# First mixture of experts: gate and up as three fp32r products, with the weights split on the fly

## The reference, cut to what matters

```python
x = x + tanh(g_xattn[0]) * xattn0(layernorm(x), ctx, ...)
# first mixture, per token: e = argmax(sigmoid(h @ router_w))
#   y = score * (silu(h @ gate_w[e]) * (h @ up_w[e])) @ down_w[e]   # 256 -> 512 -> 256
x = x + tanh(g_ffn[0]) * moe0(layernorm(x), router_w, gate_w, up_w, down_w)
x = x + tanh(g_xattn[1]) * xattn1(layernorm(x), ctx, ...)
x = x + tanh(g_ffn[1]) * moe1(layernorm(x), ...)    # 16-head attention, then 16 experts, top 6
```

## Time and profile before

| | us |
|---|---|
| median of 3 runs | 767.51 (766.88 to 768.69) |
| profiled execution, its own time | 770.28 |
| its span | 768.4 |
| PE busy in the span | 739.2 (96%) |
| DVE, ACT, POOL busy | 422.9, 343.3, 249.8 |
| mean granted TensorE clock | 0.984 of full |

### The profile page before, as it was taken

One profiled execution on the slowest core, in us unless ns is written; L12 is line 12 of the kernel. 1 busy time (PEld: TensorE's weight loads), 2 busy tenths in 40 slices (PEclk: granted clock), 3 DMA queues, 4 the chain that ended last, 5 costly groups with the idle time before them and its releaser, 6 DMA issues.

```text
span 768.4 us, 13498 instructions
## 1 busy us (share of the span) xinstructions
PE 739.2 (96%) x4623; PEld 604.2 (79%) x4624; DVE 422.9 (55%) x775; ACT 343.3 (45%) x815; POOL 249.8 (33%) x347
## 2 busy tenths in 40 slices
PE   8999999999889989999999999999999999999998
PEld 6887656666567768899889988998878888888886
DVE  6887552121568864544544454436555656566665
ACT  5888122222358863544544545445442233223223
POOL 3324140000535574622132221312324444434430
PEclk9999899999889999999999999999999999999999
DMA  8970021110300010010101101100014443343331
GB/s 293 418 313 2 28 89 32 51 41 28 123 1 2 2 35 12 25 55 22 35 20 55 34 20 34 53 30 20 9 38 124 116 119 99 116 122 96 118 100 55
DMA packets 24742, 57.38 MB, mean 75 GB/s; under 512 B 3568, under 2 KB 13296, under 8 KB 23680
## 3 DMA queue, kind: packets, MB, share of 16 engines
q1 hardware_dynamic: 23936, 54.77, 21.8%
q0 software_dynamic: 768, 2.10, 0.9%
HBM read 50.76 MB, written 6.09 MB: 74 GB/s over the span
## 4 chain that ended last, share of the span: by engine, by line
PE 83%; ACT 6%; DVE 6%; POOL 2%; DMA 1%; issue 1%; SPq 0%; DVEq 0%; POOLq 0%; ACTq 0%
PE PS L343 16%; PE PS L345 15%; PE PS L344 15%; PE PS L1730 7%; PE PS L1451 7%; PE PS L1466 3%; PE PS L457 3%; PE PS L492 2%; PE PS L501 2%; PE PS L463 2%; PE PS L1736 2%; PE PS L1418 2%; PE PS L514 1%; POOL Z L838 1%; ACT x_probT L663 1%
## 5 line engine op out<-in xcount | busy, mean ns | idle before, releaser
L343 PE MATMUL PS<-tTh,wh 128*128 128x512 f32 x200 | 78.3, 392 | 0.8 <-DVE tTl L653 0.5
L1242 ACT ACTIVATE hhh<-hh 128x512 fp32r<-128x512 f32 x50 | 31.6, 632 | 104.6 <-DVE hh L1268 94.7
L345 PE MATMUL PS<-tTh,wl 128*128 128x512 f32 x200 | 77.9, 389 | 0.0
L344 PE MATMUL PS<-tTl,wh 128*128 128x512 f32 x200 | 77.8, 389 | 0.0
L653 DVE TENSOR_TENSOR hhl<-hh,hhh 128x512 fp32r<-128x512 f32 x50 | 52.4, 1047 | 35.4 <-ACT hhh L1242 35.4
L1841 ACT ACTIVATE sm<-sm,nmx 128x128 f32<-128x128 f32 x128 | 49.7, 391 | 37.8 <-DVE nmx L1904 37.8
L1334 POOL CAST wh<-wraw 128x512 fp32r<-128x512 f32 (+1 forms) x50 | 26.1, 523 | 109.9 <-PE PS L345 109.9
L653 DVE TENSOR_TENSOR oTl<-PS,oTh 128x512 fp32r<-128x512 f32 x32 | 22.1, 692 | 71.5 <-ACT oTh L1835 71.5
L1336 POOL TENSOR_TENSOR wl<-wraw,wh 128x512 fp32r<-128x512 f32 (+1 forms) x50 | 58.0, 1160 | 8.4 <-POOL wh L1334 7.9
L1944 POOL CAST ah<-araw 128x512 fp32r<-128x512 f32 (+1 forms) x32 | 16.2, 506 | 134.6 <-PE PS L345 134.6
L1451 PE MATMUL PS<-WE,xsT 128*128 x120 | 56.2, 593 | 0.6 <-ACT xsT L1524 0.6
(11 more groups left out here) (265 smaller groups left out, 1840.7 us busy)
## 6 DMA issues: line engine op xcount, KB each, us to landing
WE<-moe SPq DMA_DIRECT2D x8, 1536.0 KB, 18.9
wraw<-moe SPq DMA_DIRECT2D x25, 384.0 KB, 3.1
araw<-attn SPq DMA_DIRECT2D x16, 384.0 KB, 3.1
cwb<-cw_d SPq DMA_DIRECT2D x20, 256.0 KB, 3.9
WX<-wx SPq DMA_DIRECT2D x4, 512.0 KB, 6.9
avraw<-attn_v SPq DMA_DIRECT2D x8, 256.0 KB, 3.1
xs_d<-zeros SPq DMA_DIRECT2D x1, 1920.0 KB, 22.3
ys_d<-y_s SPq DMA_DIRECT2D x15, 128.0 KB, 1.7
```

The lines of the kernel that those rows point to most:

```text
L343: nc.tensor.matmul(out, wh_, xh_, start=first, stop=False, **kw)
L344: nc.tensor.matmul(out, wh_, xl_, start=False, stop=False, **kw)
L345: return nc.tensor.matmul(out, wl_, xh_, start=False, stop=last, **kw)
L1242: nc.scalar.activation(hhh[half][:, :], hh[half][:, :], ACT.Copy).then_inc(s.hi_done, 1)
```

## The change

Gate and up of every slot become three fp32r products each: high x high, low x high (the slot's columns split into `xsT` and `xsTl`) and high x low (weights split into `wgh` and `wgl`). ScalarE rounds the next slot's weights to `wgh` (four copies of 128 x 512 a slot), and VectorE and GpSimd subtract to get `wgl` (two pieces each in a loop slot). `wgh` and `wgl` have one buffer for gate and one for up, each of two pieces c. The down product stays fp32. Buffers move so that the new ones fit, and SyncE's first two loads of `xs_s` wait for the first four `keys_values` as well.

```diff
...
         e = ExitStack()
-        xs_s = [sb(f"xs_s{i}", [P, D], where=e) for i in range(2)]
-        xsT = [sb(f"xsT{i}", [P, C, P], where=e) for i in range(2)]
+        xsT = [sb(f"xsT{i}", [P, C, P], F32R, e) for i in range(2)]
         gs2 = sb("gs", [P, 2, I0], where=e)
...
         perm = gs2[:, :, :].rearrange("p a n -> p (a n)").rearrange("p (b s) -> p b s", b=B)
-        hs = sb("hs", [P, I0], where=e)
-        hT = sb("hT", [P, I0 // P, P], where=e)
-        y_s = [sb(f"y_s{i}", [P, D], where=e) for i in range(2)]
         kms8 = sb("kms8", [P, B], where=e)
...
         V1 = sb("V1", [P, B, XH, XD + 1], where=e)
...
+        xsTl = [sb(f"xsTl{i}", [P, C, P], F32R, e) for i in range(2)]
+        wgh = [sb(f"wgh{i}", [P, C, I0], F32R, e) for i in range(2)]
...
+        xs_s = [sb(f"xs_s{i}", [P, D], where=e) for i in range(2)]
+        hs = sb("hs", [P, I0], where=e)
+        hT = sb("hT", [P, I0 // P, P], where=e)
+        y_s = [sb(f"y_s{i}", [P, D], where=e) for i in range(2)]
+        wgl = [sb(f"wgl{i}", [P, C, I0], F32R, e) for i in range(2)]
         e.close()
...
             place_read, ids_done, perm_done, h_ready, ht_done, ht_ready, d_done, y_ready = (sem("e_" + k) for k in ("place_read", "ids_done", "perm_done", "h_ready", "ht_done", "ht_ready", "d_done", "y_ready"))
+            xt_low, w_high = sem("e_xt_low"), sem("e_w_high")
...
+            w_low = [sem(f"e_w_low{i}") for i in range(2)]
             sums_done, experts_done, zeroed = sem("e_sums_done"), sem("e_experts_done"), sem("e_zeroed")
...
-            def up(e, par, mat, done):
-                w = WE[:, bass.ds(e, 1), mat * C * I0:(mat + 1) * C * I0].rearrange("p a (c n) -> p (a c) n", c=C)
+            def up(j, par, mat, done):
...
+                out = PS[:, 2 * mat + par, :]
                 for c in range(C):
-                    m = nc.tensor.matmul(PS[:, 2 * mat + par, :], xsT[par][:, c, :], w[:, c, :], start=(c == 0), stop=(c == C - 1))
+                    pe.wait_ge(s.w_high, 4 * j + 2 * mat + c + 1)
+                    nc.tensor.matmul(out, xsT[par][:, c, :], wgh[mat][:, c, :], start=(c == 0), stop=False)
+                    if mat == 0 and c == 0:
+                        pe.wait_ge(s.xt_low, j + 1)
+                    nc.tensor.matmul(out, xsTl[par][:, c, :], wgh[mat][:, c, :], start=False, stop=False)
+                for c in range(C):
+                    pe.wait_ge(s.w_low[(mat + c) % 2], 2 * j + mat + 1)
+                    m = nc.tensor.matmul(out, xsT[par][:, c, :], wgl[mat][:, c, :], start=False, stop=(c == C - 1))
                 m.then_inc(done, 1)
...
             def tile(j, par, i):
-                e = pe.value_load(ex[0:1, bass.ds(j, 1)], min_val=0, max_val=E0 - 1)
                 pe.wait_ge(s.xt_ready, j + 1)
-                up(e, par, 0, s.g_done)
+                up(j, par, 0, s.g_done)
                 if is_first(j):
-                    up(e, par, 1, s.u_done)
+                    up(j, par, 1, s.u_done)
                     pe.wait_ge(s.ctx_in, 16 * C)
...
                 if not is_last(j):
                     columns(1 - par, i + 3 - par)
-                up(e, par, 1, s.u_done)
+                up(j, par, 1, s.u_done)
                 if not is_second(j):
...
+        def expert_columns(e, mat, c):
+            a0 = (mat * C + c) * I0
+            return WE[:, bass.ds(e, 1), a0:a0 + I0].rearrange("p a n -> p (a n)")
...
+        def low_weights(eng, e, mat, c, done):
+            eng.tensor_tensor(wgl[mat][:, c, :], expert_columns(e, mat, c), wgh[mat][:, c, :].bitcast(F32), ALU.subtract).then_inc(done, 1)
...
         def key_columns(act, i0, i1):
...
             def tile(j, par, i):
+                e = None if is_last(j) else expert(j + 1)
                 act.wait_ge(s.g_done, j + 1)
...
                 if is_first(j):
+                    weights(e, 0)
+                    act.wait_ge(s.u_done, 1)
+                    weights(e, 1)
                     hidden_columns(0)
-                elif not is_second(j):
+                    columns(1, 1)
+                    return
+                if not is_second(j):
                     hidden_columns(j - 1)
                 if not is_last(j):
                     columns(j + 1, 1 - par)
...
+                    weights(e, 0)
+                    act.wait_ge(s.u_done, j + 1)
+                    weights(e, 1)
...
+            def expert(j):
+                return act.value_load(ex[0:1, bass.ds(j, 1)], min_val=0, max_val=E0 - 1)
...
+            def weights(e, mat):
...
+                for c in range(C):
+                    nc.scalar.activation(wgh[mat][:, c, :], expert_columns(e, mat, c), ACT.Copy).then_inc(s.w_high, 1)
...
+            act.wait_ge(s.experts_done, 1)
+            act.wait_ge(s.w_in, 16 * E0)
+            e = expert(0)
+            weights(e, 0)
+            weights(e, 1)
             columns(0, 0)
...
+            def low_columns(j, par):
+                dve.wait_ge(s.xt_ready, j + 1)
+                split_lo(xsTl[par][:, :, :].rearrange("p c s -> p (c s)"), PS[:, 5, 0:D], xsT[par][:, :, :].rearrange("p c s -> p (c s)")).then_inc(s.xt_low, 1)
...
+            def expert(j):
+                return dve.value_load(ex[0:1, bass.ds(j, 1)], min_val=0, max_val=E0 - 1)
...
+            def low_gates(j, e):
+                for c in range(C if is_first(j) else 1):
+                    dve.wait_ge(s.w_high, 4 * j + c + 1)
+                    low_weights(v, e, 0, c, s.w_low[c])
...
+            def low_ups(j, e):
+                for c in range(0 if is_first(j) else 1, C):
+                    dve.wait_ge(s.w_high, 4 * j + c + 3)
+                    low_weights(v, e, 1, c, s.w_low[1 - c])
...
             def tile(j, par, i):
+                e = None if is_last(j) else expert(j + 1)
+                if not is_first(j) and not is_last(j):
+                    low_columns(j + 1, 1 - par)
                 dve.wait_ge(s.u_done, j + 1)
...
                 v.tensor_tensor(hs[:, :], gs[par][:, :], PS[:, 2 + par, :], ALU.mult).then_inc(s.h_ready, 1)
+                if not is_last(j):
+                    low_gates(j + 1, e)
                 if is_first(j):
...
                     output_rows(0, 0, 0)
+                    low_columns(1, 1)
+                    low_ups(1, e)
                     normalise_keys(dve, 0, MOST, 1)
-                elif not is_second(j):
+                    return
+                if not is_second(j):
                     output_rows(j - 1, 1 - par, i + 1)
...
-            keys_values(0, 4, False)
+                if not is_last(j):
+                    low_ups(j + 1, e)
...
+            dve.wait_ge(s.experts_done, 1)
+            e = expert(0)
+            low_gates(0, e)
+            keys_values(0, 1, False)
+            low_columns(0, 0)
+            low_ups(0, e)
+            keys_values(1, 4, False)
             slots(dve, tile)
...
             for b in range(B):
                 nc.gpsimd.indirect_dma_start(xs_d, bass.IndirectOffsetOnAxis(pos[:, b:b + 1], 0), FX[:, b, :], None).then_inc(s.scattered, 16)
+            def low_parts(j):
+                e = pool.value_load(ex[0:1, bass.ds(j, 1)], min_val=0, max_val=E0 - 1)
+                pool_wait(pool, s.w_high, 4 * j + 2)
+                low_weights(nc.gpsimd, e, 0, 1, s.w_low[1])
+                pool_wait(pool, s.w_high, 4 * j + 3)
+                low_weights(nc.gpsimd, e, 1, 0, s.w_low[1])
...
+            def tile(j, par, i):
+                if not is_last(j):
+                    low_parts(j + 1)
+                if is_first(j):
+                    keys_power(0, MOST, 1)
...
             def keys_power(b0, b1, group):
...
-            keys_power(0, MOST, 1)
+            pool.wait_ge(s.experts_done, 1)
+            pool.wait_ge(s.u_done, 1)
+            slots(pool, tile)
...
             sp.wait_ge(s.scattered, 16 * B)
+            sp.wait_ge(s.kv_done, CTX)
             load(1, 1)
```

## The result

The changed kernel took 763.18 us in the median of 7 runs (759.18 to 763.93), the kernel before 770.36 in the median of 7 on the same chips (766.88 to 771.31): ratio 0.993, 95% interval 0.9904 to 0.9955. By this ratio it is 5.4 us less, between 3.5 and 7.4; the two medians alone lie 7.2 apart. It is not the quotient of the two medians, from which it differs by up to 0.0023.) The forecast was 6.5 less, and 761.0, counted from a median of 767.5, where the seven runs of the kernel before now have 770.4.

What follows compares the result with a forecast made beforehand. TensorE's own work was taken as the bound: 12 slots x (5.81 - 5.20 - 0.03) = 7.0 us, first slots -0.8, last up product +0.3, a gain of 6.5 off 767.5, giving 761.0; range 758.5 to 766.5.

Steps and rivals of the forecast that it cites:

- What bounds the kernel, and what the products cost: Loop slots: TensorE's own work is the period, 5.81 us; gate and up fall from 3.43 to 2.72.
- forecast floor of 5.20: TensorE's work in one loop slot after the change: 5.20 us, between 5.10 and 5.28, against 5.81.
- ScalarE, VectorE and GpSimd hidden in the loop: Loop slots: rounding copies and subtractions finish before TensorE needs the pieces, with little room, 0.1 to 0.3 us for gate.
- price of late pieces: Loop slots: 0.03 us a slot off the gain, a stall of 0.1 us in every third slot.
- T: Time zero within a loop slot, where the gate product ends and the turns start; 128.49 us in the slot traced.
- The rival with the port: Loop: GpSimd's second subtraction starts ahead of waiting VectorE; period 6.65 us, time 778, slower; chance 0.10.
- The first slots: Slots 0 to 2: splitting in the open and VectorE's queue make slot 2's gate 0.8 us later, bounds 0 and 2.
- ahead of the waits, where the engines are idle: Argument against the no-change rival (766 to 768, chance 0.10): register loads of 0.3 us on two engines cost nothing there.
- two of the signs: Signs of being right: slot 2's gate ends 0.5 to 1.5 us later, slot 14's about 6 earlier.
- Behind the slots: After the slots stage: nothing changes but its time.
- The clock rival: Slots 1 and 2: TensorE idles and the granted clock falls, 1.5 us a fall, 762.5 to 764; chance 0.10.
- +0.3 for the end: Last slot's up product: a gain of 0.3 us added to the sum.

Runs made afterwards that it cites:

- split_once: Changed kernel with weights split for slot 0 alone, every slot using those of slot 0's expert: 759.06 us against 767.62 for the kernel before, ratio 0.9893.
- fp32_split_kept: Changed kernel with gate and up as single fp32 products again, all splitting and TensorE's waits kept: 769.86 us against 767.62 for the kernel before, ratio 1.0037.
- all_on_vector: Changed kernel with all four subtractions of a slot on VectorE, none on GpSimd: 760.00 us against 767.62 for the kernel before, ratio 0.9896.
- late_keys: Changed kernel with VectorE's scaling of the first six key tiles moved from behind slot 0 to the last slot: 760.72 us against 767.62 before, ratio 0.9919.

## Why the prediction was right, and where it was off

- **What bounds the kernel, and what the products cost.** Right. The fp32r steps are 0.23 apart and the first behind the transposes 0.31 (140.58 to 140.89). The forecast floor of 5.20 is 5.17 (split_once), and fp32_split_kept shows that nothing else gains.
- **ScalarE, VectorE and GpSimd hidden in the loop.** Right for the products themselves. The price of late pieces was put at 0.03 a slot, as a stall ahead of a low product, and is 0.08 (all_on_vector against the changed kernel), nearly all of it elsewhere. GpSimd's second piece was to be ready at about 5.9 after T and comes at 6.4 in ten of the twelve slots, each of its subtractions having waited for one of VectorE's; its product needs it at 6.8, but the register load of `down`, which the prediction let stay without a price, stands behind that wait. Where GpSimd is first, VectorE's piece came 0.55 behind it, as in the earlier trace rows, and not 0.69 by the whole instruction of which the Trainium skill (SBUF — State Buffer, "Who interferes with whom") speaks: at 121.82 GpSimd began, 1.27 long, and VectorE's, issued at 121.89, ended at 123.64.
- **The rival with the port.** GpSimd did not keep the port for a second piece with VectorE waiting; VectorE's longest subtraction was 1.76, one of GpSimd's and its own rest. The rival's time of 778 was far off.
- **The first slots.** This term failed: 0.8 us were forecast, with bounds of 0 and 2, and 2.3 are lost. Two steps of it were too short. In slot 0, `hs` was put 9.0 behind the expert numbers (106.0 against 97.05) and came at 10.1. ScalarE's first copy came 1.3 behind them, not 0.85, and VectorE's register load for slot 1, "ahead of the waits, where the engines are idle", lies ahead of `hs` on an engine that is not idle: it idled 0.75 us there, and the chain that ended last gives the load and its register steps 0.5 of it. Keeping slot 0 in fp32 took 1.2 back. In slot 2, the piece behind GpSimd's was forecast at 117.3 and came at 118.4, by the same hold-up a little later. The named holder, the keys' scaling, was only one of two; late_keys alone gave nothing. So two of the signs that the prediction named for being right did not come: slot 2's gate was to end 0.5 to 1.5 us later and ended 2.3 later, and slot 14's was to end about 6 earlier and ended 4.5 earlier.
- **Behind the slots.** "Nothing changes but its time" holds for the code and not for one execution of it: the clock gives or takes up to 4 us (106.3 to 110.5). The sum of 6.5 for the slots is 4.7 measured, and the spans' difference of 6.9 met the forecast by luck. The clock rival was placed wrongly: between 111 and 180 us the granted clock was 1.00, though TensorE stood for 1.17 us; the falls come at 85 to 93, at 199 to 222 and at 272 to 284 us, in either kernel.

The sum in the end: 7.0 for the loop is 6.8; -0.8 for the first slots is -2.3; +0.3 for the end is +0.2.

## What to carry to other kernels

Swapping an fp32 product for three fp32r products gains what the steps say, if every other engine's chain in the loop fits under the shorter period; lay that chain out from the trace, engine by engine, before trusting busy shares. Include what stands behind each wait in an engine's queue: a piece can be in time for its product and still hold up the register load behind it. Work that is hidden in the loop is in the open in the first iterations, register loads too, and there two holders can hide each other, so that taking away either shows nothing. Compare a stage from mark to mark and runs at equal mean clock before you put a difference of spans down to a change.

## What the runs showed of the hardware that was not expected

- Two subtractions with both inputs in SBUF, on VectorE and GpSimd, cost each other more than the time gained by sharing them out: asked for at one time, both are done after 1.83 us (142.86 to 144.69), where VectorE alone does two in 1.29. Four on VectorE alone (0.68 each) gave slots of 5.17 us, two and two gave 5.25.
- A register load on TensorE's queue that starts 1.28 us behind a slot's start instead of 0.67 delays the weights behind it: from its start to the first of them it took 0.76 us.
- The mean granted clock of a run of the kernel before lay between 0.984 and 0.997, and its span between 769.5 and 762.0 with it; where kernels were profiled, the falls sit in the same stages, among them the two at 200 to 222 us, and the second of these was absent in one profile of the changed kernel and there in the next, without any edit.
